# Routed rows of 258 numbers in place of 321: each expert computes its rows' scores from its own column of the gate

## The reference, cut to what matters

```python
logits = x_flat @ gate_weight.T             # 2048 x 64, x_flat is the normalised h
scores = sigmoid(logits)
sfc = scores + e_bias                       # only for choosing
...                                         # best 4 of 8 groups, then the best 8 experts
topk_w = take_along_axis(scores, topk_idx)
topk_w = topk_w / (topk_w.sum(-1) + 1e-20) * 2.5
...
xe[expert, pos] = x[token]                  # at most CAP = 256 rows for one expert
h = silu(xe @ w1.T) * (xe @ w3.T)           # 256 -> 128, per expert
ye = h @ w2.T                               # 128 -> 256
out = segment_sum(ye[expert, pos] * topk_w) # back to the tokens, plus a shared expert
```

## Time and profile before

| | |
|---|---|
| median of 3 runs | 1498.23 us (1497.69 to 1503.76) |
| the profiled execution | 1498.51 us, of which the span of the core is 1496.8 us |
| busy: PE, PEld, DVE, ACT, POOL | 79%, 45%, 47%, 38%, 21% |
| blocks phase | about 45 to 862 us |
| router phase ends | 1323.7 us |
| experts phase | 1323.7 us to the end |
| DMA, whole run | 101.05 MB, mean 68 GB/s |

### The profile page before, as it was taken

The page is one execution under the profiler, slowest core; times in us unless marked ns, Lnnn a source line. Parts: engine busy times, 40 slices in busy tenths (PEclk is TensorE's granted clock), DMA queues, the critical chain, the costliest instruction groups (busy, mean ns, idle before and its releaser), DMA issues. The chain is left out here.

```text
span 1496.8 us, 16771 instructions
## 1 busy us (share of the span) xinstructions
PE 1182.2 (79%) x4789; PEld 673.4 (45%) x4789; DVE 706.6 (47%) x1941; ACT 574.7 (38%) x925; POOL 315.7 (21%) x321
## 2 busy tenths in 40 slices
PE   2656999999999999999998654559999665337762
PEld 2432444444444444444444343426665543125552
DVE  1215556644556644556644147547664576112221
ACT  1234445555445555445552211316555100014341
POOL 6700000000000000000000002010000157727664
PEclk9777999999999999999999867859999568759997
DMA  1020001211011111011111100285430022139996
GB/s 16 7 86 0 24 16 60 74 67 39 22 45 67 67 39 60 28 60 52 39 39 39 48 8 8 85 176 113 95 74 1 24 88 74 59 113 219 226 219 125
DMA packets 58500, 101.05 MB, mean 68 GB/s; under 512 B 11690, under 2 KB 38772, under 8 KB 58194
## 3 DMA queue, kind: packets, MB, share of 16 engines
q1 hardware_dynamic: 38274, 59.80, 14.9%
q0 software_dynamic: 20176, 40.65, 10.2%
HBM read 59.40 MB, written 53.00 MB: 75 GB/s over the span
## 5 line engine op out<-in xcount | busy, mean ns | idle before, releaser
L428 PE MATMUL b_ring<-b_H,b_w 128*128 128x512 f32 x512 | 224.8, 592 | 0.0
L428 PE MATMUL b_ring<-b_X1T,b_w 128*128 128x512 f32 x512 | 223.5, 595 | 0.0
L622 POOL TENSOR_TENSOR b_rstd<-b_veps,b_mhalf 128x4 f32<-128x4 f32 x32 | 32.6, 1017 | 707.1 <-DVE b_veps L69 707.1
L428 PE MATMUL b_ring<-XT,b_wqkv 128*128 128x512 f32 x384 | 174.7, 599 | 7.3 <-DMA b_wqkv<-in_wqkv 7.3
L428 PEld LDWEIGHTS b_ring<-b_X1T,b_w 128*128 128x128 f32 x512 | 96.4, 191 | 116.3 <-issue 109.6
L428 PEld LDWEIGHTS b_ring<-b_H,b_w 128*128 128x128 f32 x512 | 96.1, 190 | 115.3 <-issue 115.3
L578 ACT ACTIVATE b_H<-b_ring,b_cur 128x512 f32<-128x512 f32 x128 | 88.0, 687 | 76.9 <-PE b_ring L428 69.8
L1405 DVE TENSOR_REDUCE a_nmax<-a_pA 128x2 f32<-128x512 f32 x128 | 84.9, 688 | 61.4 <-PE a_pA L1266 60.6
L428 PEld LDWEIGHTS b_ring<-XT,b_wqkv 128*128 128x128 f32 x384 | 71.4, 192 | 86.1 <-issue 78.2
L679 DVE RECIPROCAL b_rec<-b_den 128x1024 f32<-128x1024 f32 x16 | 104.8, 6553 | 0.5
L1386 ACT ACTIVATE a_ET<-a_pB 128x512 f32<-128x512 f32 x128 | 75.0, 597 | 54.3 <-PE a_pB L1287 52.1
(11 more groups left out here) (282 smaller groups left out, 1855.0 us busy)
## 6 DMA issues: line engine op xcount, KB each, us to landing
xe<-b_nil POOLq DMA_DIRECT2D x16, 1284.0 KB, 5.3
x_wt<-in_wexp SPq DMA_DIRECT2D x32, 384.0 KB, 4.5
x_rows<-xe SPq DMA_DIRECT2D x32, 321.0 KB, 5.0
b_w<-in_w SPq DMA_DIRECT2D x8, 1024.0 KB, 5.4
a_right<-qparts SPq DMA_DIRECT2D x32, 192.0 KB, 5.2
a_left<-qparts SPq DMA_DIRECT2D x32, 192.0 KB, 5.3
b_wqkv<-in_wqkv SPq DMA_DIRECT2D x4, 768.0 KB, 4.7
qparts<-q_part SPq DMA_DIRECT2D x24, 128.0 KB, 2.0
```

The source lines that it names most:

```text
L428: last = pe.matmul(bank[:, :], lhsT(k), rhs(k), start=(k == 0), stop=(k == n_k - 1))
```

## The change

A row keeps the 256 numbers of the token, the token's number, and one number more: the factor 2.5 / (sum of the token's scores), the reciprocal that DVE had computed anyway. The 64 weights are no longer written. The expert's own column of the gate (256 numbers, 2 for each partition) comes with its weights. PE multiplies the expert's transposed rows by that column (two row tiles by two halves of the depth: four products of 128x128 by 128x1), ACT takes the sigmoid, and DVE multiplies it by the factor in the row to get `share`. Rows in the tile `nil`, in `xe` and in `rows` become 1032 bytes; a partition's weights go from 3072 to 3080 bytes. The two buffers `pW` take the last two banks of PSUM.

```diff
-XW = D + 1 + NEXP
+XW = D + 2
...
-                link(dve.reciprocal(wrec[:, :], wsum2[:, :]))
-                link(dve.tensor_tensor(wfull[:, :, :], w[:, :, :], wrec[:, :].unsqueeze(2).to_broadcast([P, TPC, NEXP]), ALU.mult))
+                dve.reciprocal(row[:, l * TPC:(l + 1) * TPC, D + 1], wsum2[:, :])
...
-                dve.tensor_tensor(row[:, l * TPC:(l + 1) * TPC, D + 1:XW], wfull[:, :, :], valid[:, :, :], ALU.mult)
...
-        WCOL = 2 * KD * HID + D
+        GCOL = 2 * KD * HID + D
+        WCOL = GCOL + KD
...
+                    for i in range(SPE):
+                        for k in range(KD):
+                            last = pe.matmul(pW[e % 2][:, i:i + 1], rowsT[:, e % RINGX, k * CAP + i * P:k * CAP + (i + 1) * P],
+                                             wt[:, e % RINGX, GCOL + k:GCOL + k + 1], start=(k == 0), stop=(k == KD - 1))
+                    last.then_inc(s_sw, 1)
                 if 2 <= s:
...
                     act.activation(sg[:, e % RINGX, :], pU[e % 2][:, 0, :], ACT.Sigmoid).then_inc(s_sg, 1)
+                    act.wait_ge(s_sw, i0 + e + 1)
+                    act.activation(score[:, e % RINGX, :], pW[e % 2][:, :], ACT.Sigmoid).then_inc(s_sc, 1)
                 if 2 <= s:
                     e = s - 2
+                    act.wait_ge(s_hm, i0 + e + 1)
                     act.wait_ge(s_y, i0 + e + 1)
...
             def addressed(s, l):
-                e = dve.value_load(erow[0:1, 0, bass.ds(RINGX * l + s, 1)], min_val=0, max_val=NEXP - 1)
...
                 dve.tensor_copy(home[:, s % RINGX, :], rows[:, s % RINGX, :, D])
-                dve.tensor_copy(share[:, s % RINGX, :], rows[:, s % RINGX, :, bass.ds(e + D + 1, 1)].rearrange("p i o -> p (i o)")).then_inc(s_hm, 1)
...
                     dve.tensor_tensor(hid[:, e % RINGX, :], sgg[:, e % RINGX, :], pU[e % 2][:, 1, :], ALU.mult).then_inc(s_hd, 1)
+                    dve.wait_ge(s_sc, n)
+                    dve.tensor_tensor(share[:, e % RINGX, :], score[:, e % RINGX, :], rows[:, e % RINGX, :, D + 1], ALU.mult).then_inc(s_hm, 1)
...
+    gates = i["L1_ffn_gate_weight"].reshape(NEXP, KD, P).transpose(0, 2, 1)
+    experts = np.concatenate([w1, w3, i["L1_ffn_w2"].transpose(0, 2, 1), gates], 2)
```

More of the change, by code:

```diff
@@ L1541, in router_phase @@
         wsum2 = sb("m_wsum2", [P, TPC])
-        wrec = sb("m_wrec", [P, TPC])
-        wfull = sb("m_wfull", [P, TPC, NEXP])
         valid = sb("m_valid", [P, TPC, NEXP])
@@ L1903, in experts_phase @@
         home = sb("x_home", [P, RINGX, SPE], I32)
+        score = sb("x_score", [P, RINGX, SPE])
         share = sb("x_share", [P, RINGX, SPE])
@@ L1914, in experts_phase @@
         pY = [pb(f"x_pY{i}", [P, SPE, D]) for i in range(2)]
+        pW = [pb(f"x_pW{i}", [P, SPE]) for i in range(2)]
         s_wt = [sem(f"x_weights{i}_loaded") for i in range(RINGX)]
@@ L1939, in experts_phase @@
         s_ye = sem("x_ye_ready")
+        s_sw = sem("x_scores_done")
+        s_sc = sem("x_scores_ready")
         block = ctx.enter_context(nc.Block())
@@ L2052, in body @@
                         last = pe.matmul(pY[e % 2][:, i, :], hid[:, e % RINGX, i * P:(i + 1) * P],
-                                         wt[:, e % RINGX, 2 * KD * HID:], start=True, stop=True)
+                                         wt[:, e % RINGX, 2 * KD * HID:GCOL], start=True, stop=True)
                     last.then_inc(s_y, 1)
@@ L2185 @@
               for n in ("w1", "w3"))
-    experts = np.concatenate([w1, w3, i["L1_ffn_w2"].transpose(0, 2, 1)], 2)
+    gates = i["L1_ffn_gate_weight"].reshape(NEXP, KD, P).transpose(0, 2, 1)
+    experts = np.concatenate([w1, w3, i["L1_ffn_w2"].transpose(0, 2, 1), gates], 2)
     heads = i["L1_attn_Wq"].transpose(0, 2, 1).reshape(KD, P // DH, DH, DH)
```

## The result

The changed kernel takes 1501.5 us (median; 1498.3 to 1504.7), the kernel before 1498.0 us in the same rounds: ratio 1.0025, 95% interval 1.0013 to 1.0036. That is +3.5 us where -1.0 us was forecast. The time lies in the range, the sign is wrong: the kernel became slower. The profiled execution has a span of 1500.8 us, 4.0 more than before.

The account below looks back on a forecast made before the run. Bound: no engine alone, but POOL's adds and the equally long buffer ring, coupled by DMA engines 97% busy. Turns -1.35, fill +1.5, router -0.34, fills -0.85 gave -1.0 us: 1497.2 us, range 1491.0 to 1506.0 us (8 in 10).

Parts of the forecast that it names:

- The turn: Experts phase, time T per expert: from 4.45 to 4.40 us, over 27 turns -1.35 us.
- The loop: Experts phase, ring of four buffers: transposes to weights issue 3.43, row load 0.53 later, landing 5.0; two turns, 8.96 us.
- the landing: Experts phase, row load from issue to landed: 5.0 us before, forecast 3.9 us.
- the bytes' 0.24 us: Experts phase: 62 KB less per turn, worth 0.24 us if the DMA engines set the pace, else 0.
- the 1.7 us of waiting: Experts phase: part of a row load's 5.0 us spent waiting among other transfers; half, 0.85 us, was to go.
- rival A: Experts phase: landing stays near 5 us, products count in full, T = 4.78 us, +8.9 us, 1507.4 us in all; chance 0.20.
- the adds' loop: Experts phase, POOL's accumulating adds: 8.90 us per two turns, sharing the queue; T therefore rounded up to 4.40 us.
- The fill: Experts phase start: two steps with new products +1.70 us, smaller first row load -0.24; together +1.5 us.
- The tail: Experts phase end: POOL's wait before the last add may hide 0.85 us; taken as 0, bounds 0 to -0.85.
- The router: Router phase: a removed step between DVE's wait for the ranks and the first scatter, -0.34 us.
- The fills: End of the blocks phase: the last fills are 18% smaller, -0.85 us, bounds 0 and -1.2 us.
- ACT, DVE: Experts phase: the added sigmoid and moved product cost nothing; without cover at most 0.38 and 0.17 us a turn.

Follow-up runs that it names:

- e7: The kernel after, unedited, run and profiled again; ratio to the kernel before 1.0002, a turn 4.622 us.
- e2: The kernel before with only the four gate-column products added, result unused, rows wide; ratio 1.0051, a turn 4.568 us.
- e12: The kernel before, row load issued ahead of the weights, waiting for the transposes and s_hm but not the down product; ratio 0.9936, a turn 4.066 us.
- e5: The kernel before with the row load issued ahead of the weights; ratio 0.9970, a turn 4.284 us.
- e8: The kernel before, unedited, run and profiled again; one run, no ratio, a turn 4.476 us.
- e4: The kernel after with the row load issued ahead of the weights; ratio 0.9953, a turn 4.253 us.
- e6: The kernel after, new products moved behind the down product and row load issued ahead of the weights; ratio 0.9898, a turn 4.147 us.
- e9: The kernel after without the products and sigmoid, score left out, gate column still loaded (3080-byte weights) but unused; ratio to the kernel before 0.9960.
- e1: The kernel after without products, sigmoid and gate column, score left out: narrow rows alone; ratio to the kernel before 0.9955, a turn 4.405 us.
- e10: The kernel after, products behind the down product, row load ahead of the weights and waiting only for s_hm; ratio to the kernel before 0.9896.
- e13: Same kernel as e10, run again in the same round as e12; ratio to the kernel before 0.9902, a turn 3.940 us.
- e11: Same kernel as e6, run again; ratio to the kernel before 0.9930, a turn 4.197 us.

## Why the prediction was wrong, point by point

*The turn: the step that failed.* The loop was read rightly: 3.43 + 0.53 + landing, and the products go into it in full (measured 0.89 us between transposes and issue, 0.85 forecast). The term that was mis-sized is the landing. The prediction took 3.9 us: the bytes' 0.24 us off in full and half of the 1.7 us of waiting gone. By the loop it was 2 x 4.574 - 4.32 - 0.53 = 4.3 us (by e7's turns without the slow one too). e2 parts it: of the 0.85 us that the later issue was to take off, 0.7 came off; of the bytes' 0.24 nothing came off beside that. T rose by 0.11 us in both pairs of profiles instead of falling by 0.05. The mechanism is rival A's, at less than its price of T = 4.78.

Two readings had spoken against A. The 97% busy DMA "has to be relieved when loads come later": the later issue did relieve it, by 0.7 us a load, but the engines were no bound (e12), and fewer bytes gave nothing beside it. And the adds' loop, for which T was rounded up to 4.40, does not stand by itself: e5 shortens it by moving a load.

From the fifth step to the last the kernel after needed 7.7 us more, where -1.35 us stood in the sum. 2.5 us of them are the turns from the eighth step on, and 5.1 lie between the fifth and the eighth. For e7 against e8 it is 5.3 us, 3.5 and 1.8. So the 7.7 come near A's 8.9 in part by the event that follows.

*One event on top, in the profile of the result.* The sixth step's rows took 6.22 us to land, PE stood 2.90 us, and its granted clock fell to half. Timeline of PE, then windows (columns as in the earlier trace rows):

```profile
1350.57 0.66 PE L2035 MATMUL x_pX<-ident,x_rows 128*128 128x128 f32 x4 [2.90 <-DMA x_rows<-xe]
1351.06 2.77 PE L2045 MATMUL x_pU<-x_rowsT,x_wt 128*128 128x256 f32 x8
1353.62 1.71 PE L2050 MATMUL x_pW<-x_wt,x_rowsT 128*128 128x1 f32 x8
1355.19 2.05 PE L2058 MATMUL x_pY<-x_wt,x_hid 128*128 128x256 f32 x4
```

```profile
1345.00:1350.50 5.50, 2.67 (x17) 2.12 (x15) 0.00 (x0) 1.41 (x5) 3.39 (x3) 1.00 0.99 204
1350.50:1354.00 3.50, 3.43 (x15) 2.97 (x15) 1.01 (x4) 0.73 (x2) 1.75 (x2) 0.70 0.63 177
1354.00:1358.00 4.00, 4.00 (x16) 3.53 (x16) 1.28 (x5) 1.09 (x4) 1.33 (x1) 0.50 0.59 66
1358.00:1362.00 4.00, 4.00 (x23) 3.51 (x23) 0.91 (x3) 1.28 (x4) 2.64 (x2) 0.91 0.77 185
```

Between the fifth and the eighth step the two profiles of the kernel after differ by 3.6 us (18.3 and 14.7, before 13.2 and 12.9), so this is not in every execution. How much of it is in the median of the result isn't known.

*The fill.* +1.5 us forecast; the fifth step begins 2.1 us later against the phase's begin (1.7 in e7). Right in kind, a little small. *The tail.* 0 forecast, with bounds 0 to -0.85; measured +0.5 and +0.6 us from the last step to the end. The bound had the wrong sign.

*The router.* The first scatter of the kernel after:

```profile
1201.07 1.10 POOL L1620 DMA_INDIRECT xe<-m_row,m_idx  x1 [29.97 <-DVE m_idx L1785]
1202.47 0.99 POOL L1620 DMA_INDIRECT xe<-m_row,m_idx  x1 [0.30 <-issue]
```

It comes 34.39 us behind the phase's begin, 36.78 before. The removed step explains 0.34 us: in e4, e6 and e9, where PE's clock was as before, it is 36.37, so 0.41 us less. The other 2.0 us are clock, not work: one set of logits ran at full clock (16 records in 2.00 us from 1182.48, against 3.68), and the transposes behind it took 1.56 us in place of 1.91. *The fills.* Median landing 4.9 us (5.3 before). From the last fill's issue to the next phase:

```profile
851.43 0.54 POOL L611 DMA_DIRECT2D xe<-b_nil  x1
860.15 0.11 POOL L844 MEMSET f_mhalf<- 128x16 f32 x1 [8.18 <-POOLq L294]
```

8.72 us, 9.20 before; over all profiles 8.65 us on average (10 narrow) against 9.28 (5 wide): -0.6 us, -0.85 forecast. *ACT, DVE.* `x_hid` has 1.1 us of idle time before it in all 31 steps together, before and after alike, as forecast.

*What was not foreseen* is the clock outside the experts phase: the attention phase, -3.3 us, next section, and the router's 2.0 us. Without them the change would have cost some 9 us, so that the time still fell into the range is luck. The sum of the two profiles: -1.8 us until the blocks phase has ended (0.5 of it the fills), +0.9 until attention begins, -3.3, router -2.2, experts +10.3: +3.9, span +4.0 (the parts are rounded).

## What to carry to other kernels

A chain of waits names one of several loops of equal length, and loops that share the transfers can lengthen each other; find every loop, and ask which one still holds when the others are relaxed. Work added between a buffer's landing and its release costs a turn that waits on that buffer, even where the engine is idle a quarter of the time; and bytes saved there pay little (0.06 us a turn in e1, nothing beside the products), while moving the load's issue ahead in the queue, or its release ahead of unrelated work, pays at once (e5, e10, e12). Take a high DMA share as waiting until a higher rate has been ruled out.

## What the runs showed of the hardware

*The end of the attention phase hangs on TensorE's clock, though the change edits nothing there.* The last products of that phase in the kernel before, then in the kernel after:

```profile
1162.66 2.08 PE L1324 MATMUL a_pC<-a_wp,a_yT 128*128 128x256 f32 x4 [0.69 <-ACT a_yT L1378]
1164.67 1.22 PE L1325 MATMUL a_pC<-a_bp,a_one 1*128 1x256 f32 x2
1165.82 2.08 PE L1324 MATMUL a_pC<-a_wp,a_yT 128*128 128x256 f32 x4
1167.82 1.22 PE L1325 MATMUL a_pC<-a_bp,a_one 1*128 1x256 f32 x2
```

```profile
1161.45 1.13 PE L1324 MATMUL a_pC<-a_wp,a_yT 128*128 128x256 f32 x4 [0.69 <-ACT a_yT L1378]
1162.51 0.69 PE L1325 MATMUL a_pC<-a_bp,a_one 1*128 1x256 f32 x2
1163.14 1.13 PE L1324 MATMUL a_pC<-a_wp,a_yT 128*128 128x256 f32 x4
1164.20 0.69 PE L1325 MATMUL a_pC<-a_bp,a_one 1*128 1x256 f32 x2
```

The instructions are the same; before, the granted clock had fallen to half (1.2 GHz) at 1162.28 us, after the change it was still full (2.4 GHz) and fell at 1167.61, when the phase was over, though PE's idle gaps ahead of them are alike in both (0.72, 0.63 and 0.69 us). All five profiles with wide rows have 2.08 or 2.07 us there and a phase of 197.7 us; all ten with narrow rows have 1.13 us and 193.4 to 194.5 us, whatever the experts phase does (e12 197.7, e13 194.4, in one round). So it goes with the rows' width. By what route is open: nothing was tried that moves the clock alone.

*The router phase has two lengths, whatever the kernel.* In all of e1 to e8 it took 175 to 182 us, in the others 151 to 154. It is not a matter of the chip alone: the runs' records name chip 13 both for e1 to e4 and for e9 to e11. In e1 DVE sat idle for 31.8 us in sum before its MAX8 instructions (L1740), and POOL's scatters, which wait for DVE's indices, have gaps of 4.4 to 8.3 us; in e9, the same router code, DVE's idle time there is 0.2 us and POOL's scatters run through. The profile names no releaser for DVE's idle time, and its cause was not looked for further.
